# Sums over the keys in the first attention layer: one fp32 product per half against two fp32r passes taken one step later

## The chip, the cores and the metric

The kernel runs on one core of one Trainium2 chip. The metric is the device time of one execution in microseconds (us). A core has a matrix engine (TensorE, PE in the profile, its weight loads PEld), a vector engine (DVE), a scalar engine (ACT), GpSimd (POOL) and a queue that issues DMA (SP). Each runs its own list of instructions in order, and they meet at semaphores only.

## The reference, cut to what matters

Two layers, each a cross attention and a feed-forward part. The change lies in the first layer's cross attention, 16 batches, 56 queries, 16 heads (8 key heads), 1500 keys:

```
q = (layernorm(x) @ Wq); k = ctx @ Wk; v = ctx @ Wv           # heads of 128
scores = einsum('bhtd,bhsd->bhts', q, k) / sqrt(128)
attn = softmax(scores, axis=-1)                                # over the 1500 keys
x = x + einsum('bhts,bhsd->bhtd', attn, v) @ Wo
```

Everything is float32. The denominator of the softmax is the sum over the 1500 keys of exp(score - maximum).

## The kernel before

The layer's work on one batch is cut into 12 steps, one for each tile of 125 keys (t = 0 to 11). The 16 heads times 56 queries are 896 columns, handled in two halves of 448. The key and value projections are folded into the queries and the output weights, so that scores are products with the 128-wide context itself.

In step t of batch b, TensorE does, in this order: the scores of the next tile t+1, half 0 (four fp32r passes of 448 columns: L792 to L795, the last of them adds minus the row's maximum); some "side jobs"; the scores of tile t+1, half 1; more side jobs; the product of the probabilities of tile t with the context, half 0 (L804, one fp32 matmul that the profile shows as two records); side jobs; the same for half 1; the rest of the side jobs. The lists `STEPS` say which side jobs stand in a step. A job M (L826, one 448-column pass) makes scores of batch b+1 for the running maximum on DVE. The jobs N and A (L842 and L843, two 512-column passes) make norms that the second layer needs: DVE multiplies their result (L738); for N, POOL adds halves (L650) and DVE reduces (L747); for A, ACT adds up with four pairs of instructions (L552). Steps 0 and 1 have the jobs "MNMAMNMA", step 2 "NMAMNMA".

ACT, in its own list, does in step t first the exponentials of tile t+1 (`exp`, L570, one for each half, from PSUM to the buffer `probs`), then other work, and last the step's two `add_up`. POOL adds the probabilities of all tiles into `acc` (L641 for tiles 0 and 1, then L644).

When a batch is done, `acc` holds for each of 125 partitions the sums over its keys. `sums` (TensorE, L812) adds over the partitions with a matrix of ones, one fp32 matmul for each half. In the program half 0 of batch b-1 stands in step 0 of batch b behind the scores of half 1, and half 1 at the head of step 1. `sums_out` (ACT, L583) copies each half to `den`, the first in step 0 behind `exp`, the second behind the first `add_up` of step 0. Then DVE inverts in steps 3 to 10 and POOL multiplies.

Scores and sums share three PSUM banks, in the cyclic order of the list `ORDER` ("S" t half are scores, "D" sums, "-" is an empty turn):

```
ORDER = [("S", 0, 0), ("S", 0, 1), ("S", 1, 0), ("S", 1, 1), ("D", 0, 0), ("D", 0, 1), ("-", 0, 0)]
ORDER += [("S", t, half) for t in range(2, NT) for half in range(2)]
```

Entry i takes bank i mod 3. `wait_bank` makes TensorE wait until what stands three entries earlier has been read: by `exp` (semaphore `probs`) for scores, by `sums_out` (semaphore `den_out`) for sums.

In what follows S(t,h) are the scores of tile t, half h; D0 and D1 are the two sums; A2 and A3 are the two jobs A of step 1; N1 is the second job N of step 0.

Of the kernel before, what the change touches and what calls it, by code (L numbers as in the profile page):

```python
# [87 lines left out]

ORDER = [("S", 0, 0), ("S", 0, 1), ("S", 1, 0), ("S", 1, 1), ("D", 0, 0), ("D", 0, 1), ("-", 0, 0)]
ORDER += [("S", t, half) for t in range(2, NT) for half in range(2)]  # L90
assert len(ORDER) % 3 == 0

# [64 lines left out]
def before_attention(nc, m, a, tag, sem):  # L157

    s = semaphores(sem, tag, LN_SEMAPHORES + ["ld_x", "ld_mask", "ld_const", "ld_ident", "ld_w0", "ld_w0_rest", "ld_wq0", "ld_wq1", "ld_wq2", "ld_wq3", "ld_w1", "ld_land", "ld_nat", "const", "ready",
                 "on_act", "on_dve", "f_hi", "g_hi", "x_hi", "mcount", "ctx_hi", "q_hi", "ctx_lo", "kept",  # L160
                 "side_pe", "side_dve"])
    with ExitStack() as ctx:
# [87 lines left out]
        @block.gpsimd  # L250
        def _(pool):
            for i in range(NLOW):
                pool.wait_ge(s.ctx_hi, 1)
                cols = slice(S // NLOW * i, S // NLOW * (i + 1))
                pool.tensor_tensor(m.clo0[:, cols], m.land[:, cols], m.chi0[:, cols].bitcast(F32), ALU.subtract).then_inc(s.ctx_lo, 1)
            pool.wait_ge(s.q_hi, 1)
            pool.tensor_tensor(m.qlo0[:, :], q_first, m.qhi0[:, :].bitcast(F32), ALU.subtract).then_inc(s.kept, 1)
            pool.wait_ge(s.q_hi, 2)
            for part in range(NXQ):
                tiles = slice(NT // NXQ * part, NT // NXQ * (part + 1))  # L260
                to, x = m.xq0[:, tiles, :].bitcast(F32), nat[:, tiles, :]
                pool.tensor_tensor(to, x, to, ALU.subtract).then_inc(s.ctx_lo, 1)
                pool.wait_ge(s.ctx_lo, NLOW + 2 * part + 1)
                pool.tensor_tensor(to, to, x, ALU.add).then_inc(s.ctx_lo, 1)

        @block.vector
        def _(dve):
# [40 lines left out]
            def make_shift():  # L308

                dve.wait_ge(s.side_dve, len(PRE_SIDE))  # L310
                dve.wait_ge(s.ld_ident, 16)
                dve.tensor_tensor(m.shift0[:, :].rearrange("p (j c) -> p j c", c=TT),
                                  m.negmax[:, :].unsqueeze(2).to_broadcast([TT, QBLK, TT]),
                                  m.ident[0:TT, 0:TT].unsqueeze(1).to_broadcast([TT, QBLK, TT]),
                                  ALU.mult).then_inc(s.kept, 1)

# [124 lines left out]
def first_attention(nc, m, a, tag, sem):  # L441

    s = semaphores(sem, tag, [
        "ld_land", "ld_nat0", "ld_nat1", "ctx_hi", "ctx_lo", "q_hi", "q_lo", "nat_hi", "xq", "shift",
        "scores", "probs", "pv", "acc", "den", "den_out", "inv", "o_raw", "o_done",
        "ld_wv", "ld_wo", "side_pe", "side_dve", "side_act", "half_sum", "sum_dve", "sum_act", "rk_pre"])
    NP = 3
    with ExitStack() as ctx:
# [11 lines left out]
        top, negmax = m.top, m.negmax  # L460
        shift = [m.shift0, sb("shift1", [TT, QW], F32R)]
        prod = [sb(f"prod{i}", [KT, 4, C], F32) for i in range(NPROD)]
# [59 lines left out]
        def _(act):  # L522
# [50 lines left out]
            def values_out(b):  # L573
# [15 lines left out]
            for b in range(B):  # L589
                for t in range(NT):  # L590
                    for tile in tile_ahead(1, b, t):
                        exp(*tile)
                    if t == 0 and b > 0:
                        sums_out(b - 1, 0)
                        norms_out(b - 1)
                    if t == 2 and b + 1 < B:
                        nat_high(b + 1)
                    if t == NT - 1:
                        if b + 2 < B:
                            query_high(b + 2)  # L600
                            context_high(b + 2, 0)
                    for n in STEP_JOBS[b, t]:
                        if JOBS[n].kind == "A":
                            add_up(n)
                        if n == first_of(b, "A") and b > 0:
                            sums_out(b - 1, 1)
                        if JOBS[n].kind == "V":
                            i = JOBS[n].i
                            act.wait_ge(s.side_pe, n + 1)
                            act.activation(m.vo[:, 2 * i:2 * i + 2, :], side[n % 3][:, :], ACT.Copy).then_inc(s.side_act, 1)  # L610
                values_out(b)
                if b + 2 < B:
                    context_high(b + 2, 1)
# [7 lines left out]
        def _(pool):  # L621
# [46 lines left out]
            def make_shift(b):  # L668

                pool.wait_ge(s.side_dve, number(job_at("T", b, 1), "MTNA"))  # L670
                need(pool, s.scores, 2 * NT * (b - 1))
                pool.tensor_tensor(shift[b % 2][:, :].rearrange("p (j c) -> p j c", c=TT),
                                   negmax[:, :].unsqueeze(2).to_broadcast([TT, QBLK, TT]),
                                   m.ident[0:TT, 0:TT].unsqueeze(1).to_broadcast([TT, QBLK, TT]),
                                   ALU.mult).then_inc(s.shift, 1)

            for b in range(B):
                for t in range(NT):
# [103 lines left out]
        def _(pe):  # L782
            def scores_half(b, t, half):
# [10 lines left out]
                pe.matmul(out, chi[b % 2][:, keys], qhi[b % 2][:, cols], start=False, stop=False)  # L794
                pe.matmul(out, m.ones_r[:, :], shift[b % 2][:, cols], start=False, stop=True).then_inc(s.scores, 1)  # L795

# [51 lines left out]
            for b in range(B):  # L848
                for t in range(NT):
# [29 lines left out]
def second_attention(nc, m, a, tag, sem):  # L879

    s = semaphores(sem, tag, [
        "ld_land", "ld_nat0", "ld_nat1", "ctx_hi", "ctx_lo", "q_hi", "q_lo", "scores", "scaled", "probs", "pv", "pv_first", "acc",
        "acc_hi", "acc_lo", "den", "inv", "o_raw", "o_done", "fold_pe", "fold_act", "fold_dve", "y_pe", "y_act"])
    LAG, NP = 2, 3
    with ExitStack() as ctx:
# [43 lines left out]
        def _(act):  # L929
# [60 lines left out]
            for i in range(KC):  # L990
                act.wait_ge(s.y_pe, i + 1)
                act.activation(land[:, HALF * i:HALF * i + HALF], slots[:, 0, i, 0:HALF], ACT.Copy).then_inc(s.y_act, 1)

# [944 lines left out]
def build(nc, a, out):  # L1938
    with ExitStack() as ctx:
# [89 lines left out]
```

## Time and profile before

| | |
|---|---|
| median of 3 runs | 2083.45 us (2082.59 to 2083.99) |
| the profiled execution | 2081.46 us, span in the trace 2079.7 us |
| first attention layer in the trace | about 71 to 1155 us, batches of about 67.6 us |
| PE busy | 2051.3 us, 99% of the span |
| DVE, ACT, POOL busy | 1576.0 us (76%), 1208.0 us (58%), 1451.0 us (70%) |

A row of the timeline gives start and duration of an instruction in us, its engine, its line, what it writes and reads, its shape; in brackets the time that the engine sat idle before it and who ended that. Matmuls are pipelined: in a dense stream the durations overlap, and the cost of one is the distance from one end to the next.

### The profile page before, as it was taken

What the parts mean: (1) busy time and instruction counts of PE and PEld (TensorE: products, weight loads), DVE (VectorE), ACT (ScalarE), POOL (GpSimd) and SP (SyncE); (2) the same over time, 40 slices, a digit from 0 to 9 for tenths busy, and PEclk for the clock granted to TensorE, in tenths of its full rate; (3) what the DMA queues carried; (4) which work ended last, traced back from release to release, by engine and by line L of the source; (5) the groups of instructions that cost most, each with busy time, mean ns of one, the idle gap of its engine ahead of it and who ended that gap; (6) DMA issues with size and microseconds to landing.
All of it is one profiled execution on the core that took longest, in us unless ns stands there. A gap on an engine that the chain in (4) does not pass through costs nothing. (4 is left out here: it accounts for less than half of the span.)

```text
span 2079.7 us, 28199 instructions
## 1 busy us (share of the span) xinstructions
PE 2051.3 (99%) x8482; PEld 1520.4 (73%) x8482; DVE 1576.0 (76%) x2489; ACT 1208.0 (58%) x4201; POOL 1451.0 (70%) x1092
## 2 busy tenths in 40 slices
PE   8999999999999999999999989999999999999999
PEld 7777777777777777777777577666666666665998
DVE  4789988898889888898886677476766676752576
ACT  4676777767776777677767347544444444432433
POOL 1688888888888888888886254678787877851221
PEclk9999999999999999999999999999999999999999
DMA  4000000000000000000010410121211111001110
GB/s 138 30 16 17 30 30 16 30 16 31 30 16 16 31 31 16 17 30 30 16 43 9 137 58 1 45 60 31 59 33 57 41 49 48 28 0 54 46 51 22
DMA packets 15289, 75.68 MB, mean 36 GB/s; under 512 B 1762, under 2 KB 2258, under 8 KB 14130
## 3 DMA queue, kind: packets, MB, share of 16 engines
q1 hardware_dynamic: 15138, 73.89, 10.9%
q8 instruction: 68, 1.11, 0.2%
q14 instruction: 83, 0.68, 0.1%
HBM read 72.97 MB, written 0.92 MB: 36 GB/s over the span
## 5 line engine op out<-in xcount | busy, mean ns | idle before, releaser
L552 ACT ACTIVATE l_prod_act<-l_prod_act 125x128 f32<-125x128 f32 x1536 | 456.3, 298 | 298.6 <-DVE l_prod_act L738 293.5
L650 POOL TENSOR_TENSOR l_prod<-l_prod 125x256 f32<-125x256 f32 x384 | 280.3, 739 | 163.9 <-DVE l_prod L738 162.7
L1009 POOL TENSOR_TENSOR l_acc<-l_acc,l_probs 125x896 f32<-125x896 f32 x160 | 346.6, 2167 | 67.9 <-ACT l_probs L946 49.5
L946 ACT ACTIVATE l_probs<-l_scaled 125x896 f32<-125x896 f32 x192 | 182.8, 952 | 302.7 <-DVE l_scaled L1031 160.6
L1031 DVE TENSOR_TENSOR l_scaled<-l_slots,rk 125x896 f32<-125x896 f32 x192 | 206.9, 1084 | 180.9 <-PE l_slots L1107 180.7
L644 POOL TENSOR_TENSOR l_acc<-l_acc,l_probs 125x896 f32<-125x896 f32 x160 | 339.8, 2124 | 0.0
L552 ACT ACTIVATION_READ_ACCUMULATOR l_prod_act<-l_prod_act 125x1 f32 x1536 | 287.6, 187 | 0.0
L714 DVE SCALAR_TENSOR_TENSOR top<-l_side,mask_bias,top 125x448 f32<-125x448 f32 x330 | 217.4, 659 | 25.7 <-PE l_side L826 17.9
L570 ACT ACTIVATE l_probs<-l_slots,mask_bias 125x448 f32<-125x448 f32 x384 | 219.5, 617 | 1.2
L1105 PE MATMUL l_slots<-l_qhi,l_clo 128*125 128x448 f32 x384 | 203.0, 529 | 0.4
L842 PE MATMUL l_side<-norm_lo,l_chi 128*125 128x512 f32 x384 | 185.1, 482 | 0.1
L842 PE MATMUL l_side<-norm_lo,chi 128*125 128x512 f32 x384 | 180.9, 471 | 0.0
L804 PE MATMUL l_psO<-l_probs,spare 125*128 125x448 f32 x384 | 176.0, 539 | 0.0
L804 PE MATMUL l_psO<-l_probs,l_nat 125*128 125x448 f32 x384 | 176.0, 539 | 0.0
L738 DVE TENSOR_TENSOR l_prod<-l_side,xq 125x512 f32<-125x512 f32 x192 | 131.9, 687 | 50.7 <-PE l_side L843 49.0
L738 DVE TENSOR_TENSOR l_prod<-l_side,spare 125x512 f32<-125x512 f32 x192 | 131.8, 687 | 39.8 <-PE l_side L843 37.2
L1123 PE MATMUL l_psO<-l_probs,nat 125*128 125x448 f32 x384 | 160.5, 539 | 0.6 <-ACT qs L958 0.3
L1123 PE MATMUL l_psO<-l_probs,l_nat 125*128 125x448 f32 x384 | 160.3, 540 | 0.4
L747 DVE TENSOR_REDUCE l_msq<-l_prod 125x4 f32<-125x256 f32 x384 | 154.2, 408 | 0.0
L843 PE MATMUL l_side<-norm_hi,chi 128*125 128x512 f32 x384 | 151.4, 394 | 0.0
L843 PE MATMUL l_side<-norm_hi,l_chi 128*125 128x512 f32 x384 | 151.4, 394 | 0.0
L1106 PE MATMUL l_slots<-l_qlo,l_chi 128*125 128x448 f32 x384 | 140.6, 366 | 0.0
(277 smaller groups left out, 4952.3 us busy)
## 6 DMA issues: line engine op xcount, KB each, us to landing
land<-in_ctxT SPq DMA_DIRECT2D x32, 750.0 KB, 4.2
l_nat<-in_ctxN SPq DMA_DIRECT2D x16, 750.0 KB
post_we<-in_experts SPq DMA_DIRECT2D x20, 384.0 KB, 3.0
spare<-in_ctxN SPq DMA_DIRECT2D x8, 750.0 KB
nat<-in_ctxN SPq DMA_DIRECT2D x8, 750.0 KB
spare<-in_wo SPq DMA_DIRECT2D x2, 2048.0 KB, 7.4
spare<-in_wqT SPq DMA_DIRECT2D x4, 512.0 KB, 7.5
mid_fac<-in_factors SPq DMA_DIRECT2D x1, 2048.0 KB, 7.9
```

The lines of the kernel that those rows point to most:

```text
L552: last = act.activation(whole, whole, ACT.Copy, accum_out=msq[:, t, 4 * g + c:4 * g + c + 1])
L570: act.activation(P[t % NP][:, HALF * i:HALF * i + HALF], bank_of("S", t, i)[0:KT, 0:HALF], ACT.Exp, bias=m.mask_bias[:, b, t:t + 1]).then_ ...
L644: pool.tensor_tensor(acc[:, :], acc[:, :], P[t % NP][:, :], ALU.add).then_inc(s.acc, 1)
L650: pool.tensor_tensor(buf[:, :, 0:C // 2], buf[:, :, 0:C // 2], buf[:, :, C // 2:C], ALU.add).then_inc(s.half_sum, 1)
L714: dve.scalar_tensor_tensor(top[:, cols], bank, bias, top[:, cols], ALU.add, ALU.max).then_inc(s.side_dve, 1)
L738: dve.tensor_tensor(to[:, :, :], bank, xt.unsqueeze(1).to_broadcast([KT, 4, C]), ALU.mult).then_inc(s.side_dve, 1)
L804: last = pe.matmul(psO[:, half, 0:HALF], nat[b % 2][:, t, :], P[t % NP][:, cols], start=t == 0, stop=t == NT - 1)
L842: pe.matmul(bank[0:KT, :], chi[b % 2][:, keys], m.norm_lo[:, cols], start=True, stop=False)
L843: last = pe.matmul(bank[0:KT, :], chi[b % 2][:, keys], m.norm_hi[:, cols], start=False, stop=True)
L1009: pool.tensor_tensor(acc[:, :], acc[:, :], P[t % NP][:, :], ALU.add).then_inc(s.acc, 1)
L1031: dve.tensor_tensor(scaled[t % 2][:, :].rearrange("p (a h q) -> p a h q", a=2, q=QS), src, rk.to_broadcast([KT, 2, H // 2, QS]), ALU.mult) ...
L1123: last = pe.matmul(psO[:, half, 0:HALF], nat[par][:, t, :], P[t % NP][:, cols], start=t == 0, stop=t == NT - 1)
```

## The change

The sums of all batches but the last are made in another way. ACT copies `acc` rounded to fp32r (`sum_high`, L583 of the changed kernel) into `qlo` of the batch that is over, in step 0 behind `exp`. POOL subtracts the rounded part from `acc` into that batch's `shift` buffer (`sum_low`), at the end of its step 0. TensorE then multiplies ones with both parts, two fp32r passes for each half in place of one fp32 matmul. D0 moves from step 0 to step 1 (behind S(2,1)), D1 from the head of step 1 to the head of step 2. `sums_out` of half 0 stands in ACT's step 1 behind `exp`, that of half 1 at the head of ACT's step 2, ahead of `exp`. In `ORDER` the sums come after S(2,1). The matrix `ones_r` and the `shift` buffers grow to fit, two waits keep the buffers safe, and semaphores that nobody waited for are gone.

```diff
-ORDER = [("S", 0, 0), ("S", 0, 1), ("S", 1, 0), ("S", 1, 1), ("D", 0, 0), ("D", 0, 1), ("-", 0, 0)]
-ORDER += [("S", t, half) for t in range(2, NT) for half in range(2)]
+ORDER = [("S", t, half) for t in range(3) for half in range(2)] + [("D", 0, 0), ("D", 0, 1), ("-", 0, 0)]
+ORDER += [("S", t, half) for t in range(3, NT) for half in range(2)]
...
+            def sum_high(b):
+
+                act.wait_ge(s.acc, (NT - 1) * (b + 1))
+                act.wait_ge(s.scores, 2 * NT * (b + 1))
+                act.activation(qlo[b % 2][0:KT, :], acc[:, :], ACT.Copy).then_inc(s.sum_hi, 1)
+
...
+                    if t == 2 and b > 0:
+                        sums_out(b - 1, 1)
                     for tile in tile_ahead(1, b, t):
                         exp(*tile)
                     if t == 0 and b > 0:
+                        sum_high(b - 1)
+                        norms_out(b - 1)
+                    if t == 1 and b > 0:
                         sums_out(b - 1, 0)
-                        norms_out(b - 1)
...
-                        if n == first_of(b, "A") and b > 0:
-                            sums_out(b - 1, 1)
...
-                    need(pool, s.den, 2 * b)
+                    need(pool, s.sum_lo, b)
...
+            def sum_low(b):
+
+                pool.wait_ge(s.sum_hi, b + 1)
+                pool.tensor_tensor(shift[b % 2][:, :], acc[:, :], qlo[b % 2][0:KT, :].bitcast(F32), ALU.subtract).then_inc(s.sum_lo, 1)
...
+                    if t == 0 and b > 0:
+                        sum_low(b - 1)
...
-                pe.wait_ge(s.acc, (NT - 1) * (b + 1))
+                cols, out = slice(HALF * half, HALF * half + HALF), bank_of("D", 0, half)[:, 0:HALF]
                 wait_bank(pe, b + 1, "D", 0, half)
-                pe.matmul(bank_of("D", 0, half)[:, 0:HALF], m.ones[0:KT, :], acc[:, HALF * half:HALF * half + HALF],
-                          start=True, stop=True).then_inc(s.den, 1)
+                if b == B - 1:
+                    pe.wait_ge(s.acc, (NT - 1) * B)
+                    pe.matmul(out, m.ones[0:KT, :], acc[:, cols], start=True, stop=True).then_inc(s.den, 1)
+                    return
+                pe.wait_ge(s.sum_lo, b + 1)
+                pe.matmul(out, m.ones_r[0:KT, :], shift[b % 2][:, cols], start=True, stop=False)
+                pe.matmul(out, m.ones_r[0:KT, :], qlo[b % 2][0:KT, cols], start=False, stop=True).then_inc(s.den, 1)
...
-                    if t == 1 and b > 0:
+                    if t == 2 and b > 0:
                         sums(b - 1, 1)
                     for half in range(2):
                         for tile in tile_ahead(1, b, t):
                             scores_half(*tile, half)
-                        if half == 1 and t == 0 and b > 0:
+                        if half == 1 and t == 1 and b > 0:
                             sums(b - 1, 0)
```

The order of ACT's instructions around steps 0 to 2 of a batch, before: `exp` of tile 1 (L570), the two copies of sums (L583), the norms (L559), `add_up` (L552, x4 is one job A), `exp` of tile 2, two `add_up`, `exp` of tile 3.

```order
L570 ACTIVATE l_probs<-l_slots,mask_bias 125x448 x2
L583 ACTIVATE l_den<-l_slots 128x448
L559 ACTIVATE rk<-l_msq 125x192
L552 ACTIVATE l_prod_act,l_msq<-l_prod_act 125x128 x4
L583 ACTIVATE l_den<-l_slots 128x448
L552 ACTIVATE l_prod_act,l_msq<-l_prod_act 125x128 x4
L570 ACTIVATE l_probs<-l_slots,mask_bias 125x448 x2
L552 ACTIVATE l_prod_act,l_msq<-l_prod_act 125x128 x8
L570 ACTIVATE l_probs<-l_slots,mask_bias 125x448 x2
```

And in the changed kernel, where the copy of a sum is L589:

```order
L570 ACTIVATE l_probs<-l_slots,mask_bias 125x448 x2
L583 ACTIVATE l_qlo<-l_acc 125x896
L559 ACTIVATE rk<-l_msq 125x192
L552 ACTIVATE l_prod_act,l_msq<-l_prod_act 125x128 x8
L570 ACTIVATE l_probs<-l_slots,mask_bias 125x448 x2
L589 ACTIVATE l_den<-l_slots 128x448
L552 ACTIVATE l_prod_act,l_msq<-l_prod_act 125x128 x8
L589 ACTIVATE l_den<-l_slots 128x448
L570 ACTIVATE l_probs<-l_slots,mask_bias 125x448 x2
```

The second copy of a sum stood in step 0 between its two `add_up`; it now stands behind both `add_up` of step 1.

TensorE's instructions at the head of step 2 in the changed kernel, from the last side job of step 1 (with the semaphores waited for): D1 in two passes, S(3,0), one job N, S(3,1).

```order
L863 MATMUL l_side<-norm_lo,chi 125x512 [waits l0_side_dve]
L864 MATMUL l_side<-norm_hi,chi 125x512
L833 MATMUL l_slots<-l_shift,ones_r 128x448 [waits l0_sum_lo,l0_probs]
L834 MATMUL l_slots<-l_qlo,ones_r 128x448
L808 MATMUL l_slots<-qhi,clo 125x448 [waits l0_den_out]
L809 MATMUL l_slots<-qlo,chi 125x448
L810 MATMUL l_slots<-qhi,chi 125x448
L811 MATMUL l_slots<-shift,ones_r 125x448
L863 MATMUL l_side<-norm_lo,chi 125x512 [waits l0_side_dve]
L864 MATMUL l_side<-norm_hi,chi 125x512
L808 MATMUL l_slots<-qhi,clo 125x448 [waits l0_den_out]
```

The same place before, with other line numbers for the same work:

```order
L842 MATMUL l_side<-norm_lo,chi 125x512 [waits l0_side_dve]
L843 MATMUL l_side<-norm_hi,chi 125x512
L792 MATMUL l_slots<-qhi,clo 125x448 [waits l0_probs]
L793 MATMUL l_slots<-qlo,chi 125x448
L794 MATMUL l_slots<-qhi,chi 125x448
L795 MATMUL l_slots<-shift,ones_r 125x448
L842 MATMUL l_side<-norm_lo,chi 125x512 [waits l0_side_dve]
L843 MATMUL l_side<-norm_hi,chi 125x512
L792 MATMUL l_slots<-qhi,clo 125x448 [waits l0_probs]
```

S(3,0) and S(3,1) waited for exponentials and now wait for the copies of D0 and D1 (`den_out`).

## Rows read from the trace of the kernel before

**Rows 1.** The page: engines over the whole span, and the granted clock in 40 slices.

```profile
PE 2051.3 (99%) x8482; PEld 1520.4 (73%) x8482; DVE 1576.0 (76%) x2489; ACT 1208.0 (58%) x4201; POOL 1451.0 (70%) x1092
...
PEclk9999999999999999999999999999999999999999
```

**Rows 2.** Windows over batches 7 and 8: stretch, length, then busy time of each engine.

```profile
544.35:611.90 67.55, 67.55 (x277) 50.76 (x276) 59.95 (x107) 48.80 (x226) 57.56 (x52) 1.00 0.07 24
611.90:679.59 67.69, 67.69 (x278) 50.83 (x276) 59.95 (x107) 48.82 (x226) 57.59 (x52) 1.00 0.07 24
```

**Rows 3.** Timeline of PE, batch 7, from S(1,1) in step 0 to step 2.

```profile
546.46 0.37 PE L795 MATMUL l_slots<-l_shift,ones_r 112*125 112x448 f32 x1
546.67 0.92 PE L812 MATMUL l_slots<-l_acc,ones 125*128 125x448 f32 x2
547.08 0.71 PE L826 MATMUL l_side<-qhi,chi 128*125 128x448 f32 x1
...
553.79 0.36 PE L795 MATMUL l_slots<-l_shift,ones_r 112*125 112x448 f32 x1
...
557.26 0.40 PE L843 MATMUL l_side<-norm_hi,l_chi 128*125 128x512 f32 x1
...
558.57 0.40 PE L843 MATMUL l_side<-norm_hi,l_chi 128*125 128x512 f32 x1
```

**Rows 4.** Timeline of PE in the second layer: sums in two fp32r passes.

```profile
1865.24 0.37 PE L1138 MATMUL l_norm<-l_acc_lo,l_one 125*128 125x448 f32 x1
1865.44 0.36 PE L1139 MATMUL l_norm<-l_acc_hi,l_one 125*128 125x448 f32 x1
```

**Rows 5.** Timeline of DVE, step 0 of batch 7, and its product for A3.

```profile
546.80 0.68 DVE L738 TENSOR_TENSOR l_prod<-l_side,xq 125x512 f32<-125x512 f32 x1
...
549.26 0.68 DVE L714 SCALAR_TENSOR_TENSOR top<-l_side,mask_bias,top 125x448 f32<-125x448 f32 x1
549.86 0.68 DVE L738 TENSOR_TENSOR l_prod<-l_side,xq 125x512 f32<-125x512 f32 x1
...
557.93 0.68 DVE L738 TENSOR_TENSOR l_prod_act<-l_side,xq 125x512 f32<-125x512 f32 x1
```

**Rows 6.** Timeline of POOL, batch 7: the half sum of N1, the first addition.

```profile
550.62 0.73 POOL L650 TENSOR_TENSOR l_prod<-l_prod 125x256 f32<-125x256 f32 x1 [2.32 <-DVE l_prod L738]
552.00 2.13 POOL L641 TENSOR_TENSOR l_acc<-l_probs 125x896 f32<-125x896 f32 x1 [0.65 <-PE l_slots L812]
```

**Rows 7.** Timeline of ACT, batch 7: copies of the sums, A3's add_up, exp of tile 3.

```profile
549.49 0.54 ACT L583 ACTIVATE l_den<-l_slots 128x448 f32<-128x448 f32 x1
549.91 0.37 ACT L559 ACTIVATE rk<-l_msq 125x192 f32<-125x192 f32 x1
...
551.89 0.54 ACT L583 ACTIVATE l_den<-l_slots 128x448 f32<-128x448 f32 x1 [0.24 <-PE l_slots L812]
...
558.64 0.31 ACT L552 ACTIVATE l_prod_act<-l_prod_act 125x128 f32<-125x128 f32 x1 [1.65 <-DVE l_prod_act L738]
...
559.84 0.61 ACT L570 ACTIVATE l_probs<-l_slots,mask_bias 125x448 f32<-125x448 f32 x1
```

**Rows 8.** Groups by form: a 896-column copy on ACT, subtraction on POOL (mean ns).

```profile
L526 ACT ACTIVATE qhi<-qs 128x896 fp32r<-128x896 f32 x7 | 6.6, 942 | 0.0
...
L633 POOL TENSOR_TENSOR qlo<-qs,qhi 128x896 fp32r<-128x896 f32 x7 | 14.8, 2114 | 0.0
```

**Rows 9.** Timeline at two places where PE waited: for ACT's L610, for ACT's exp.

```profile
1150.18 0.57 ACT L610 ACTIVATE spare<-l_side 128x512 f32<-128x512 f32 x1
...
1150.81 0.18 PEld L842 LDWEIGHTS l_side<-norm_lo,l_chi 128*125 128x125 f32 x1 [0.82 <-ACT spare L610]
1150.81 0.49 PE L842 MATMUL l_side<-norm_lo,l_chi 128*125 128x512 f32 x1
...
74.12 0.47 PE L792 MATMUL l_slots<-qhi,clo 128*125 128x448 f32 x1
```

**Rows 10.** Timeline of PE between the layers: its longest idle time there.

```profile
1208.76 0.96 PE L1532 MATMUL mid_bk<-ident,mid_xn 112*128 112x112 f32 x8 [1.66 <-DVE mid_xn L1240]
```

More of the change, by code:

```diff
@@ L159, in before_attention @@
     s = semaphores(sem, tag, LN_SEMAPHORES + ["ld_x", "ld_mask", "ld_const", "ld_ident", "ld_w0", "ld_w0_rest", "ld_wq0", "ld_wq1", "ld_wq2", "ld_wq3", "ld_w1", "ld_land", "ld_nat", "const", "ready",
-                 "on_act", "on_dve", "f_hi", "g_hi", "x_hi", "mcount", "ctx_hi", "q_hi", "ctx_lo", "kept",
+                 "on_act", "on_dve", "f_hi", "g_hi", "x_hi", "mcount", "ctx_hi", "q_hi", "ctx_lo",
                  "side_pe", "side_dve"])
@@ L256, in _ @@
             pool.wait_ge(s.q_hi, 1)
-            pool.tensor_tensor(m.qlo0[:, :], q_first, m.qhi0[:, :].bitcast(F32), ALU.subtract).then_inc(s.kept, 1)
+            pool.tensor_tensor(m.qlo0[:, :], q_first, m.qhi0[:, :].bitcast(F32), ALU.subtract)
             pool.wait_ge(s.q_hi, 2)
@@ L311, in make_shift @@
                 dve.wait_ge(s.ld_ident, 16)
-                dve.tensor_tensor(m.shift0[:, :].rearrange("p (j c) -> p j c", c=TT),
+                dve.tensor_tensor(m.shift0[0:TT, :].rearrange("p (j c) -> p j c", c=TT),
                                   m.negmax[:, :].unsqueeze(2).to_broadcast([TT, QBLK, TT]),
                                   m.ident[0:TT, 0:TT].unsqueeze(1).to_broadcast([TT, QBLK, TT]),
-                                  ALU.mult).then_inc(s.kept, 1)
+                                  ALU.mult)
             dve.memset(m.ones[:, :], 1.0).then_inc(s.const, 1)
@@ L444, in first_attention @@
         "ld_land", "ld_nat0", "ld_nat1", "ctx_hi", "ctx_lo", "q_hi", "q_lo", "nat_hi", "xq", "shift",
-        "scores", "probs", "pv", "acc", "den", "den_out", "inv", "o_raw", "o_done",
+        "scores", "probs", "pv", "acc", "sum_hi", "sum_lo", "den", "den_out", "inv", "o_raw", "o_done",
         "ld_wv", "ld_wo", "side_pe", "side_dve", "side_act", "half_sum", "sum_dve", "sum_act", "rk_pre"])
@@ L460, in first_attention @@
         top, negmax = m.top, m.negmax
-        shift = [m.shift0, sb("shift1", [TT, QW], F32R)]
+        shift = [m.shift0, sb("shift1", [KT, QW], F32R)]
         prod = [sb(f"prod{i}", [KT, 4, C], F32) for i in range(NPROD)]
@@ L632, in query_low @@
                     pool.wait_ge(s.scores, 2 * NT * (b - 1))
+                    pool.wait_ge(s.den, 2 * (b - 1))
                 pool.tensor_tensor(qlo[b % 2][:, :], m.qs[:, b, :, :].rearrange("p h q -> p (h q)"),
@@ L671, in make_shift @@
                 need(pool, s.scores, 2 * NT * (b - 1))
-                pool.tensor_tensor(shift[b % 2][:, :].rearrange("p (j c) -> p j c", c=TT),
+                need(pool, s.den, 2 * (b - 1))
+                pool.tensor_tensor(shift[b % 2][0:TT, :].rearrange("p (j c) -> p j c", c=TT),
                                    negmax[:, :].unsqueeze(2).to_broadcast([TT, QBLK, TT]),
@@ L794, in scores_half @@
                 pe.matmul(out, chi[b % 2][:, keys], qhi[b % 2][:, cols], start=False, stop=False)
-                pe.matmul(out, m.ones_r[:, :], shift[b % 2][:, cols], start=False, stop=True).then_inc(s.scores, 1)
+                pe.matmul(out, m.ones_r[0:TT, 0:KT], shift[b % 2][0:TT, cols], start=False, stop=True).then_inc(s.scores, 1)
             def values_half(b, t, half):
@@ L882, in second_attention @@
         "ld_land", "ld_nat0", "ld_nat1", "ctx_hi", "ctx_lo", "q_hi", "q_lo", "scores", "scaled", "probs", "pv", "pv_first", "acc",
-        "acc_hi", "acc_lo", "den", "inv", "o_raw", "o_done", "fold_pe", "fold_act", "fold_dve", "y_pe", "y_act"])
+        "acc_hi", "acc_lo", "den", "inv", "o_raw", "o_done", "fold_pe", "fold_act", "fold_dve", "y_pe"])
     LAG, NP = 2, 3
@@ L991, in _ @@
                 act.wait_ge(s.y_pe, i + 1)
-                act.activation(land[:, HALF * i:HALF * i + HALF], slots[:, 0, i, 0:HALF], ACT.Copy).then_inc(s.y_act, 1)
+                act.activation(land[:, HALF * i:HALF * i + HALF], slots[:, 0, i, 0:HALF], ACT.Copy)
         @block.gpsimd
@@ L1966, in build @@
             for_first = lambda n, sh, dt: only.enter_context(nc.sbuf_tensor(n, sh, dt))
-            m.ones_r = for_first("ones_r", [TT, KT], F32R)
+            m.ones_r = for_first("ones_r", [C, C], F32R)
             m.mask_bias = for_first("mask_bias", [KT, B, NT], F32)
@@ L1974, in build @@
             m.top, m.negmax = for_first("top", [KT, QW], F32), for_first("negmax", [TT, QBLK], F32)
-            m.shift0 = for_first("shift0", [TT, QW], F32R)
+            m.shift0 = for_first("shift0", [KT, QW], F32R)
             m.xq = for_first("xq", [KT, NT, C], F32)
```

## The prediction, made before the changed kernel ran

> **What bounds the kernel now.** I read the page first. TensorE is busy for 99% of the span and the granted clock stands in its top tenth throughout, which is the 2.4 GHz level [rows 1]. The windows over two batches of the first layer show the same closer: 67.55 us of PE in 67.55 us, 67.69 in 67.69, against at most 59.95 on DVE, 57.6 on POOL and 48.8 on ACT [rows 2]. So in this stage a microsecond of TensorE's own work that goes is a microsecond gained, but a microsecond in which TensorE waits is also lost, since it has no other slack to take it from. The timelines of one batch (batch 7; the two windows show how alike batches are) then say who would be late where.
>
> I count TensorE by ends. S(1,1) ends at 546.46 + 0.37 = 546.83. The side job behind the sum ends at 547.08 + 0.71 = 547.79 and is itself one pass [rows 3]. A pass of 448 columns in a stream costs 0.20 [rows 4]. That leaves 547.79 - 0.20 - 546.83 = 0.76 for the fp32 sum; I use 0.75.
>
> **What the change takes away.** Two passes of 0.20 and 0.21 come in place of 0.75: a sum of this very shape, 125x448 with ones, stands in the second layer at that spacing [rows 4]. I take 0.41 for both, so 0.34 is saved on each half. There are 15 batches with two halves: 30 x 0.34 = **10.2 us less**. With the ends read 0.04 otherwise it is 9 to 11.4.
>
> What this price would be by a rule: the Trainium skill ("FP8 and Floating Point Precision", TensorE Precision Notes) says a true fp32 product takes four passes through the array. Four passes at this trace's 0.204 would be 0.82, the saving 0.41 a half and 12.3 us in all. The row gives 0.76, so the rule counts a little too much here, and the sum goes by the row.
>
> POOL's first addition waited for the old sum, 0.65 us [rows 6]; POOL was idle there and this frees nothing on TensorE.
>
> **What it adds on ACT and POOL.** The copy of `acc` on ACT has the size of one at 0.94 us, POOL's subtraction the size of one at 2.11 [rows 8]. Neither engine is the bound: POOL goes from 57.6 to 59.7 in a batch of 67.6. What matters is when they end. If no one waited, they would cost nothing. ACT trades a copy of 0.54 for 0.94 in step 0.
>
> **First new wait: D0 for the low part.** TensorE wants D0 right behind S(2,1). Before, S(2,1) ended at 553.79 + 0.36 = 554.15 [rows 3]; with the two fp32 sums ahead of it gone, 554.15 - 1.50 = 552.65. The low part needs two things. First, the high part: ACT begins it at 549.49, where the copy of D0 stood [rows 7], and ends it 0.94 later, 550.43. Second, POOL must be through with the half sum of N1, which stands ahead in its list. Before, DVE's product for N1 began at 549.86 and ended at 550.54, and POOL began at 550.62 [rows 5, 6]. Now TensorE brings N1 0.75 earlier, but DVE has a chain of its own: the product at 546.80 and then M1, A0, M2, N1, back to back at 0.60 each (549.26 to 549.86) [rows 5]. So N1's product begins at 546.80 + 4 x 0.60 = 549.20, ends at 549.88; POOL's half sum runs from 549.96 to 550.69, and the subtraction to 550.69 + 2.11 = 552.80. That is later than the 552.65 at which TensorE comes.
>
> What a wait costs beyond its length shows where TensorE waited before. ACT's L610 ended at 1150.75, the weight load and the matmul began at 1150.81; behind exp a 448-column pass took 0.47 from there [rows 9]. So the first pass ends 0.06 + 0.47 = 0.53 behind the end of its producer, against 0.20 in a stream. D0's first pass: 552.80 + 0.53 = 553.33 in place of 552.85, **0.48 lost** per batch. Bounds: if DVE has no backlog, the low part is 0.2 earlier, and 0.3 is lost; if POOL is 0.2 later, 0.7. If the copy alone decided, 550.43 + 2.11 + 0.53 = 553.07, still 0.22 lost; nothing is lost only if the end of the low part comes 0.5 earlier than I reckon.
>
> **Second new wait: S(3,1) for the copy of D1.** This is the large one. In `ORDER` S(3,0) now comes three entries behind D0 and S(3,1) three behind D1, so both wait for `den_out`. S(3,0) is safe: D0 ends near 553.5; ACT copies it when it has done, from 550.43 on, the norms (0.37), two `add_up` (1.20 each, 558.64 to 559.84) and two halves of exp (0.61 each) [rows 7], so by 555.0 with the copy itself, while TensorE wants the bank after 557. For S(3,1), ACT must have copied D1 out, and in ACT's list that copy stands behind both `add_up` of step 1. The second of these belongs to A3, the last side job of step 1. All the work from A3 on is therefore in series. Before, A3 ended on TensorE at 557.26 + 0.40 = 557.66; DVE multiplied from 557.93; ACT's `add_up` began at 558.64 and the next instruction of ACT, exp, at 559.84 [rows 3, 5, 7]. That is 2.18 behind the end of A3. The copy takes this place and lasts 0.54 [rows 7], S(3,1)'s first pass ends 0.53 behind it: 2.18 + 0.54 + 0.53 = 3.25 behind A3. D1 itself is long done, 0.41 behind A3, so it is only the copy's place in ACT's list that matters.
>
> TensorE would need much less: from A3's end to the end of the job N behind S(3,0) it took 558.57 + 0.40 - 557.66 = 1.31 [rows 3]. With D1 (0.41) ahead and the first pass of S(3,1) (0.20), 1.92. **Lost: 3.25 - 1.92 = 1.33** per batch. The wait is tied to the same batch's A3 and not to how early TensorE is, so the 0.7 gained before does not cover it. Bounds: the chain behind A3 depends on DVE's backlog; with the product begun at once, 0.05 behind A3 rather than 0.27, the loss is 1.1; with 0.2 more on ACT it is 1.5.
>
> While it waits, TensorE's own later work is queued behind: a job M and A, the values of tile 2, and so all of step 2. exp of tile 3 comes behind the copy and is 0.54 late against A3, but its first consumer is in step 3. Nothing of this gives time back, because TensorE stays dense after it.
>
> A rule that speaks for less: the Trainium skill ("TensorE: Matmul & The Clock Gate", Step-by-step) says TensorE pulls weight loads ahead of matmuls in flight. If it did so ahead of a wait, the load would be over and a pass would end in about 0.37 in place of 0.47, 30 x 0.10 = 3 us less lost in all. At the wait in rows 9 the weight load itself begins only when ACT has ended, so the trace does not bear that out for a load whose matmul waits, and I keep 0.47.
>
> **The sum.** Per batch -0.68 + 0.48 + 1.33 = +1.13; 15 of them are +17.0. The last of these has no M jobs and is a little different (its step 1 is shorter, so D0 comes sooner against the low part); I add 0.3 for it: **+17.3 us**. Against the profiled execution, 2081.46 + 17.3 = 2098.8. The median of the runs lies 2.0 above that execution, 2083.45, so I say 2100.7 for the runs. The wider `ones_r` fill, the dropped semaphores and the bounds of the other instructions lie in the preamble and beside other work, or are no work: nothing.
>
> **The rivals.**
>
> Only the saving counts (ends on the other side). One mechanism: the copy of D1 gets ahead of TensorE. It does if ACT reaches it by 1.92 - 0.53 - 0.54 = 0.85 behind A3, where the rows say 2.18; and the low part is in time. Time: 2083.45 - 10.2 = 2073.2. For it speaks that the list entry "-" and the steps leave the banks much room elsewhere; against it, ACT's list in the order shown, in which both `add_up` stand ahead. I give it 0.07.
>
> Only S(3,1) waits; the low part is in time because DVE's or POOL's chain in step 0 is half a microsecond shorter than reckoned. -10.2 + 15 x 1.33 = +9.8: 2093.2. For it: the margin is 0.15 of bare time plus the restart. Against: even ACT's copy alone would leave 0.22. Chance 0.13, the near half of it inside my range.
>
> The second wait is about half of what I reckon (ACT's `add_up` for A3 overlaps more), 0.65 a batch: the sum is then -10.2 + 15 x (0.3 + 0.65) = +4, within reach of no change if the first is nothing. Chance 0.06.
>
> More is late: POOL's 2.11 us pushes its additions and half sums, DVE waits for half sums, TensorE for DVE, another 0.5 a batch: +24.8, 2108. POOL had 0.65 and 2.32 idle in step 0 and 1 [rows 6], which takes the 2.11 up; or the clock falls after waits of over 1 us. Against the clock: TensorE sat 1.66 idle between the layers and the granted clock stayed up [rows 1, 10]. Chance 0.08.
>
> Both waits as reckoned: 0.66.
>
> **How the numbers follow.** The likeliest gives 2100.7; with its bounds (losses 1.1 and 0.3 to 1.5 and 0.7, saving 9 to 11.4) it runs from 2083.45 + 21.3 - 11.4 = 2093.4 to 2083.45 + 33.3 - 9 = 2107.8. The range 2093 to 2106 takes these ends almost whole and half of the case with one wait; outside are the other side, the halved wait and the worse case, some 0.2. A change within 0.2%, 4.2 us, is about what a measurement of this kernel can't tell from none. Slower by more: 0.66 + 0.13 + 0.08 and part of the halved case, 0.89; same 0.04; faster 0.07.
>
> **What would show it.** Right: PE's passes of the sums 0.20 apart, twice 30 of them; in each batch a PE idle time ahead of the first pass of S(3,1) (L808) with ACT's copy L589 as its end, about 1.3 us of lost end-to-end time, 15 times, and a short one ahead of D0 (L833) that POOL's subtraction ends; batches of some 68.7 us. Wrong: no wait at L808 and batches of 66.9 would mean that the copy of D1 is earlier than ACT's list lets me think. No wait at L833 alone would mean that DVE's chain in step 0 is shorter. If the time went up by over 25, a wait elsewhere, on DVE's side banks or on POOL, would have to show.

## The result

The change makes the kernel slower: 2106.5 us median (2102.8 to 2107.0, 4 runs) against 2083.0 us (2081.4 to 2084.0, 4 runs), ratio 1.0107 with a 95% interval of 1.0095 to 1.012. The medians are 23.5 us apart, 20 to 25 us by the interval, where I had said 17.3. The 2106.5 stands at the very top of my range of 2093 to 2106: half a microsecond above it as a time, and just inside it by the ratio (1.0107, where 2106 over the 2083.45 that I reckoned from is 1.0108). The profiled execution took 2106.46 us, with a span of 2104.6 us.

The profile's page for the changed kernel says little: TensorE is busy for 6 us more, 98% of the span in place of 99%.

```profile
PE 2057.4 (98%) x8482; PEld 1519.0 (72%) x8482; DVE 1576.2 (75%) x2489; ACT 1219.0 (58%) x4216; POOL 1481.4 (70%) x1107
```

Windows cut at the ends of the values' products show where the time went. Columns: stretch, length, busy time (and number of instructions) of PE, PEld, DVE, ACT, POOL, granted clock, DMA share, GB/s. First the kernel before, steps 0, 1, 2 and 3 to 11 of batch 7:

```profile
544.05:550.43 6.38, 6.38 (x27) 4.67 (x26) 5.69 (x12) 6.03 (x23) 4.08 (x5) 1.00 0.26 99
550.43:556.99 6.56, 6.56 (x28) 4.85 (x27) 5.13 (x9) 5.37 (x27) 4.51 (x4) 1.00 0.05 21
556.99:562.61 5.62, 5.62 (x25) 4.30 (x24) 5.02 (x10) 3.97 (x15) 4.48 (x4) 1.00 0.01 3
562.61:611.60 48.99, 48.99 (x204) 36.94 (x203) 44.11 (x80) 33.44 (x165) 44.50 (x39) 1.00 0.05 17
```

Then the changed kernel, the same four stretches of batch 7, and the whole of batches 7 and 8, which answer to [rows 2]:

```profile
554.55:560.57 6.02, 6.02 (x24) 4.13 (x24) 5.60 (x12) 5.76 (x21) 4.07 (x5) 1.00 0.26 94
560.57:567.21 6.64, 6.45 (x27) 4.76 (x27) 5.12 (x9) 5.81 (x29) 6.32 (x5) 1.00 0.07 31
567.21:574.56 7.35, 6.31 (x27) 4.59 (x26) 5.09 (x10) 5.04 (x20) 4.67 (x5) 1.00 0.01 2
574.56:623.57 49.01, 49.01 (x203) 36.94 (x203) 44.15 (x80) 32.89 (x161) 44.51 (x39) 1.00 0.05 17
554.55:623.57 69.02, 67.78 (x277) 50.43 (x277) 59.97 (x108) 49.50 (x227) 59.56 (x53) 1.00 0.07 23
623.57:692.62 69.05, 67.85 (x278) 50.49 (x277) 59.95 (x108) 49.53 (x227) 59.61 (x53) 1.00 0.07 23
```

Steps 3 to 11 have not changed by more than 0.02 us. The batch is 69.03 us on the mean of the two in place of 67.62: +1.41 us, 15 times, is 21.2. (The sums are remade 15 times, once for each batch that has a predecessor.) Step by step: step 0 lost an fp32 product of 0.75 and is only 0.36 shorter; step 1 had 0.75 taken away and 0.41 put in, and is 0.08 longer; step 2 had 0.41 put in and is 1.73 longer. So TensorE lost 0.39 + 0.42 + 1.32 us in three places, of which I had named two.

The timeline of PE in the changed kernel, batch 7, shows the places (L847 is a side job M, L863 and L864 are a side job's passes, L820 the values, L811 the end of scores, L833 and L834 a sum, L808 the start of scores):

```profile
557.16 0.37 PE L847 MATMUL l_side<-qhi,chi 128*125 128x448 f32 x1
557.43 0.49 PE L863 MATMUL l_side<-norm_lo,l_chi 128*125 128x512 f32 x1
557.77 0.40 PE L864 MATMUL l_side<-norm_hi,l_chi 128*125 128x512 f32 x1
558.16 0.99 PE L820 MATMUL l_psO<-l_probs,l_nat 125*128 125x448 f32 x2
...
563.17 0.36 PE L811 MATMUL l_slots<-l_shift,ones_r 112*125 112x448 f32 x1
563.73 0.45 PE L833 MATMUL l_slots<-shift,ones_r 125*128 125x448 f32 x1 [0.19 <-POOL shift L657]
564.01 0.36 PE L834 MATMUL l_slots<-qlo,ones_r 125*128 125x448 f32 x1
...
567.71 0.37 PE L833 MATMUL l_slots<-shift,ones_r 125*128 125x448 f32 x1
567.92 0.37 PE L834 MATMUL l_slots<-qlo,ones_r 125*128 125x448 f32 x1
...
569.18 0.40 PE L864 MATMUL l_side<-norm_hi,l_chi 128*125 128x512 f32 x1
570.62 0.47 PE L808 MATMUL l_slots<-l_qhi,l_clo 128*125 128x448 f32 x1 [1.04 <-ACT l_den L589]
```

ACT and POOL in the same stretch: the copy of the values, the rounded copy of `acc`, A3's `add_up`, the copy of D1; N1's half sum and the subtraction.

```profile
557.03 0.98 ACT L577 ACTIVATE qs<-l_psO,valid 128x896 f32<-128x896 f32 x1
...
559.98 0.94 ACT L583 ACTIVATE qlo<-l_acc 125x896 fp32r<-125x896 f32 x1
...
568.86 0.31 ACT L552 ACTIVATE l_prod_act<-l_prod_act 125x128 f32<-125x128 f32 x1 [1.65 <-DVE l_prod_act L754]
...
570.05 0.52 ACT L589 ACTIVATE l_den<-l_slots 128x448 f32<-128x448 f32 x1
```

```profile
560.75 0.74 POOL L663 TENSOR_TENSOR l_prod<-l_prod 125x256 f32<-125x256 f32 x1 [1.96 <-DVE l_prod L754]
561.44 2.14 POOL L657 TENSOR_TENSOR shift<-l_acc,qlo 125x896 fp32r<-125x896 f32 x1
```

Read from the end of one matmul to the end of the next. **S(3,1):** the copy of D1 ends at 570.57, L808 starts at 570.62 and ends at 571.09; in a stream it would have ended at 569.58 + 0.20, so 1.31 is lost. **D0:** the subtraction ends at 563.58, L833 starts at 563.73 and ends at 564.18 in place of 563.53 + 0.20: 0.45. **Step 0, values of tile 0:** ACT's copy of the last batch's values out of the same PSUM ends at 558.01; the product ends at 559.15, and not at 558.17 + 0.75 = 558.92: 0.23. Just before, the side job's first pass ends at 557.92 and not at 557.53 + 0.23 = 557.76: 0.16. The weight loads name what ended two of these waits, DVE's first M (L727) at 557.43 and ACT's copy of D1 (L589) at 570.62. At 558.13 the view names only the issue, so that the copy of the values ended that wait is read from the times alone; e2 tests it:

```profile
557.43 0.18 PEld L863 LDWEIGHTS l_side<-norm_lo,l_chi 128*125 128x125 f32 x1 [0.29 <-DVE top L727]
558.13 0.30 PEld L820 LDWEIGHTS l_psO<-l_probs,l_nat 125*128 125x128 f32 x2 [0.41 <-issue]
...
570.62 0.18 PEld L808 LDWEIGHTS l_slots<-l_qhi,l_clo 128*125 128x125 f32 x1 [1.49 <-ACT l_den L589]
```

And the view of waits over the first layer says that it is every batch that has a predecessor (in total, times, longest):

```profile
PEld l_slots L808 <- ACT l_den L589: 21.9, 15, 1.5
PEld l_slots L833 <- issue: 8.3, 15, 0.9
PEld l_psO L820 <- issue: 6.7, 15, 1.0
```

Read in the same way in all 15 batches, D0 loses 0.42 to 0.45 us and S(3,1) 1.28 to 1.32 in the first 14. In the last one, which has no M jobs, they lose 0.76 and 1.17.

The two profiled executions are 24.9 us apart (spans of 2104.6 and 2079.7). Most of the 3.7 us beyond 21.2 does not lie in the changed steps. The last section has it.

### The profile page after: what moved, and what is told of

It is laid out like the page before. It is cut to its first block and busy times, and to the rows that moved or that the text cites. A ratio compares the mean times of both kernels' runs of the same rounds, so it can differ in the third digit from the quotient of the medians.

```text
span 2104.6 us, 28244 instructions
## 1 busy us (share of the span) xinstructions
PE 2057.4 (98%) x8482; PEld 1519.0 (72%) x8482; DVE 1576.2 (75%) x2489; ACT 1219.0 (58%) x4216; POOL 1481.4 (70%) x1107
## 5 line engine op out<-in xcount | busy, mean ns | idle before, releaser
L552 ACT ACTIVATE l_prod_act<-l_prod_act 125x128 f32<-125x128 f32 x1536 | 456.1, 298 | 304.5 <-DVE l_prod_act L754 299.3
L552 ACT ACTIVATION_READ_ACCUMULATOR l_prod_act<-l_prod_act 125x1 f32 x1536 | 287.5, 187 | 0.0
L570 ACT ACTIVATE l_probs<-l_slots,mask_bias 125x448 f32<-125x448 f32 x384 | 219.6, 617 | 9.8 <-PE l_slots L811 9.7
L863 PE MATMUL l_side<-norm_lo,l_chi 128*125 128x512 f32 x384 | 185.7, 484 | 0.1
L863 PE MATMUL l_side<-norm_lo,chi 128*125 128x512 f32 x384 | 181.4, 472 | 0.0
L820 PE MATMUL l_psO<-l_probs,l_nat 125*128 125x448 f32 x384 | 176.5, 540 | 0.6 <-ACT qs L577 0.6
L820 PE MATMUL l_psO<-l_probs,spare 125*128 125x448 f32 x384 | 176.5, 541 | 0.0
L763 DVE TENSOR_REDUCE l_msq<-l_prod 125x4 f32<-125x256 f32 x384 | 154.5, 409 | 0.0
L864 PE MATMUL l_side<-norm_hi,chi 128*125 128x512 f32 x384 | 151.5, 394 | 0.0
L864 PE MATMUL l_side<-norm_hi,l_chi 128*125 128x512 f32 x384 | 151.3, 394 | 0.0
```

Of the source, the lines that this page charges most:

```text
L552: last = act.activation(whole, whole, ACT.Copy, accum_out=msq[:, t, 4 * g + c:4 * g + c + 1])
L570: act.activation(P[t % NP][:, HALF * i:HALF * i + HALF], bank_of("S", t, i)[0:KT, 0:HALF], ACT.Exp, bias=m.mask_bias[:, b, t:t + 1]).then_ ...
L820: last = pe.matmul(psO[:, half, 0:HALF], nat[b % 2][:, t, :], P[t % NP][:, cols], start=t == 0, stop=t == NT - 1)
L863: pe.matmul(bank[0:KT, :], chi[b % 2][:, keys], m.norm_lo[:, cols], start=True, stop=False)
L864: last = pe.matmul(bank[0:KT, :], chi[b % 2][:, keys], m.norm_hi[:, cols], start=False, stop=True)
```

## The experiments

Eight kernels, each timed in five rounds beside the kernel before (2082.6 us median in the first four, 2083.4 with the last four).

**e1, the copy of D1.** D1 is made in step 1, ahead of the second half of the values, and copied out between the two `add_up` of step 1.

```diff
-                    if t == 2 and b > 0:
-                        sums_out(b - 1, 1)
...
                             add_up(n)
+                            if t == 1 and b > 0 and JOBS[n].i == 2:
+                                sums_out(b - 1, 1)
...
-                    if t == 2 and b > 0:
-                        sums(b - 1, 1)
...
+                    if t == 1 and b > 0:
+                        sums(b - 1, 1)
                     values_half(b, t, 1)
```

> The changed kernel with one difference: D1 is made in step 1, ahead of the second half of the values of tile 1, and ACT copies it out between the two add_up of step 1; S(3,1) then finds its bank free. My theory (the place of D1's copy in ACT's list costs 1.31 us per batch, 15 times): 19.7 us less than the changed kernel, batches of 67.7 us in place of 69.03, about 2085 to 2087 us. Rival (the loss comes from the extra copy on ACT and the extra subtraction on POOL, wherever the sums stand): no difference, 2103 to 2107 us. No idle time of PE that ends by L589 should be left.

Measured: 2086.9 us (2084.5 to 2087.5), ratio 1.0017 (1.0008 to 1.0026). Steps 1 and 2 and the whole of batch 7:

```profile
551.27:558.31 7.04, 6.86 (x29) 5.15 (x29) 5.52 (x10) 6.21 (x30) 6.72 (x6) 1.00 0.06 27
558.31:563.93 5.62, 5.62 (x24) 4.30 (x24) 4.71 (x9) 4.09 (x15) 4.31 (x4) 1.00 0.01 3
...
545.24:612.92 67.68, 67.49 (x278) 50.51 (x277) 59.97 (x108) 49.41 (x227) 59.59 (x53) 1.00 0.07 24
```

Step 2 is back at 5.62, step 1 has taken over the 0.41 of the product. 1.34 us of batch 7 (1.27 of batch 8) and 19.6 us of the median went with the place of D1 and its copy; the product had to move with the copy, which reads it. ACT and POOL do the same work (49.41 and 59.59 us busy against 49.50 and 59.56). The rival, that the additional work costs in itself wherever the sums stand, is out.

**e2, the copy of the values.**

```diff
+                        if t == NT - 1 and JOBS[n].kind == "A" and JOBS[n].i == NBLK_A - 1:
+                            values_out(b)
                         if JOBS[n].kind == "A":
                             add_up(n)
...
-                values_out(b)
                 if b + 2 < B:
                     context_high(b + 2, 1)
```

> The changed kernel with one difference: ACT copies out the values of a batch ahead of the last add_up of step 11 and not behind it. Theory (with D0 gone from step 0, the first values product of step 0 waits for this copy, 0.23 us of 0.39 lost there, the other 0.16 a wait for DVE): step 0 is 0.2 to 0.4 us shorter, 3 to 6 us less than the changed kernel, about 2100 us. Rival (step 0 is longer than reckoned because the fp32 sum that was there cost only 0.35 us): no difference.

Measured: 2100.6 us (2099.2 to 2105.3), ratio 1.0092 (1.0076 to 1.0107). This interval overlaps with the changed kernel's (1.0095 to 1.012), and the medians are 5.9 us apart where the trace gives 3 (0.21 a batch, 15 times). So the time alone does not size this step; the trace does. Step 0 is 5.80 in place of 6.02 us:

```profile
551.44:557.24 5.80, 5.80 (x25) 4.22 (x24) 5.60 (x12) 5.80 (x21) 4.10 (x5) 1.00 0.26 94
```

These 0.22 us are the wait for the copy, read above as 0.23; the 0.16 for DVE stays.

**e3, the low part.** ACT rounds `acc` ahead of `exp`, and POOL subtracts ahead of its half sum for N1.

```diff
+                    if t == 0 and b > 0:
+                        sum_high(b - 1)
                     for tile in tile_ahead(1, b, t):
                         exp(*tile)
                     if t == 0 and b > 0:
-                        sum_high(b - 1)
                         norms_out(b - 1)
...
                             halve(n)
-                    if t == 0 and b > 0:
-                        sum_low(b - 1)
+                            if t == 0 and b > 0 and JOBS[n].i == 0:
+                                sum_low(b - 1)
```

> The changed kernel with two moves: ACT makes the rounded copy of acc ahead of exp of tile 1, and POOL subtracts ahead of its half sum for the second job N of step 0. Theory (D0 waits for the low part, 0.45 us lost per batch): step 1 is 0.45 us shorter, 6.7 us less than the changed kernel, about 2098 to 2100 us, and L833 has no idle time before it. Rival (the wait at D0 is paid back at S(3,1), whose wait ends by ACT's copy at a time that does not depend on D0): no difference. Theory says that wait hangs on A3, which moves with D0, so all of it is gained.

Measured: 2099.7 us (2097.9 to 2100.3), ratio 1.0081 (1.0067 to 1.0095). Step 1 and step 2:

```profile
557.53:563.74 6.21, 6.21 (x27) 4.85 (x27) 5.13 (x9) 5.81 (x29) 5.93 (x5) 1.00 0.07 31
563.74:571.06 7.32, 6.28 (x26) 4.58 (x26) 5.09 (x10) 5.03 (x19) 4.44 (x4) 1.00 0.01 2
```

Step 1 gains 0.43 and step 2 stays (7.32 against 7.35): the wait at S(3,1) hangs on A3 of the same batch and does not eat what is gained ahead of it.

**e4, all three.** The moves of e1, e2 and e3 together.

> All three moves of the runs before at once. Theory: the waits are gone and the saving of 0.68 us per batch is left, less at most 0.16 for the side bank that DVE holds in step 0: 7.8 to 10.2 us less than the kernel before, 2073 to 2076 us, batches of 66.95 to 67.1 us. Rival (ACT's and POOL's additional work costs in itself): 2083 or more.

Measured: 2074.5 us (2073.0 to 2075.3), ratio to the kernel before 0.9961 (0.9948 to 0.9973): 8 us faster than before, and the best kernel of this study.

```profile
541.00:546.79 5.79, 5.79 (x24) 4.21 (x24) 5.59 (x12) 5.79 (x21) 4.84 (x6) 1.00 0.27 96
546.79:553.40 6.61, 6.61 (x29) 5.22 (x29) 5.54 (x10) 6.08 (x30) 6.03 (x6) 1.00 0.08 33
553.40:559.02 5.62, 5.62 (x25) 4.30 (x24) 4.72 (x9) 4.08 (x15) 4.24 (x4) 1.00 0.01 3
...
541.00:608.03 67.03, 67.03 (x277) 50.66 (x277) 60.00 (x108) 49.30 (x227) 59.63 (x53) 1.00 0.07 24
608.03:675.10 67.07, 67.07 (x277) 50.72 (x277) 59.96 (x108) 49.35 (x227) 59.67 (x53) 1.00 0.07 24
```

A batch is 67.05 on the mean of the two, 0.57 below 67.62. The saving of 0.68 less the 0.16 of DVE's side bank, which no move touches, would be 0.52: they agree to 0.05.

**e5, a control: the kernel before with e2's move.**

> The kernel before with one difference: ACT copies the values of a batch out ahead of the last add_up of step 11. Theory (the fp32 sum D0 in step 0 hid the wait for this copy, so there was none): no difference, 2081 to 2084 us, step 0 stays 6.38 us. Rival (the copy cost TensorE time before too, and the gain of the same move in the changed kernel has nothing to do with D0): some 3 us less.

Measured: 2083.4 us (2081.6 to 2085.1), ratio 0.9998 (0.9989 to 1.0007), step 0 at 6.38. The copy of the values costs nothing as long as the fp32 product of D0 stands ahead of the values:

```profile
546.84:553.22 6.38, 6.38 (x26) 4.68 (x26) 5.69 (x12) 6.29 (x25) 4.07 (x5) 1.00 0.26 100
```

**e6 and e7, the price of the product with and without a wait behind it.** Both have one fp32 product of the rounded part for each pair of passes; e6 is otherwise the changed kernel, e7 is otherwise e4. They leave the low part out of the denominators, so they serve to price the product only.

```diff
-                pe.matmul(out, m.ones_r[0:KT, :], shift[b % 2][:, cols], start=True, stop=False)
-                pe.matmul(out, m.ones_r[0:KT, :], qlo[b % 2][0:KT, cols], start=False, stop=True).then_inc(s.den, 1)
+                pe.matmul(out, m.ones[0:KT, :], qlo[b % 2][0:KT, cols].bitcast(F32), start=True, stop=True).then_inc(s.den, 1)
```

> The changed kernel with each pair of passes of a sum replaced by one fp32 product of ones and the rounded part; the low part stays out of the denominators, its subtraction and the waits stay. Theory: D0 costs 0.34 us more per batch, D1 stands ahead of the wait for its own copy, which hangs on A3's add_up and not on D1, so D1's 0.34 is hidden: 5.1 us more than the changed kernel (batches of 69.37 us), 2108 to 2111 us. Rival (TensorE's own work counts everywhere): 10.2 us more, batches of 69.7, 2113 to 2116 us.

> The kernel with all three moves, again with one fp32 product of the rounded part for each pair of passes (the low part stays out of the denominators). Theory: there is no wait there that could hide it, so both halves count, 0.68 us per batch, 10.2 us more than with two passes: about 2084 to 2085 us, batches of 67.7 us. Rival (the two passes save less than 0.34 a half in place): less than that.

Measured: e6 2109.9 us (2109.3 to 2110.7), ratio 1.0125 (1.0112 to 1.0139), e7 2085.1 us (2083.3 to 2087.4), ratio 1.0007 (0.9998 to 1.0016). First e6, steps 1 and 2; then e7, step 1 and the whole batch:

```profile
561.70:568.68 6.98, 6.79 (x27) 4.78 (x27) 5.12 (x9) 5.91 (x29) 6.57 (x5) 1.00 0.05 22
568.68:576.03 7.35, 6.63 (x27) 4.61 (x26) 5.09 (x10) 5.04 (x19) 4.44 (x4) 1.00 0.01 2
```

```profile
551.94:559.26 7.32, 7.32 (x29) 5.24 (x29) 5.56 (x10) 6.21 (x30) 6.37 (x6) 1.00 0.06 27
...
546.15:613.85 67.70, 67.69 (x277) 50.74 (x277) 59.97 (x108) 49.41 (x227) 59.56 (x53) 1.00 0.07 24
```

In e6 step 1 is 0.34 longer, step 2 is 7.35 as in the changed kernel though its product is 0.34 longer: behind it TensorE waits anyway. e6's batches are 69.36 and 69.38 us, 0.34 longer. In e7 both products count: 7.32 against 6.61 in step 1, which holds both. So the saving that the change was to bring is real and of the size reckoned, and in the changed kernel the half that D1 saves was spent on a longer wait.

**e8, DVE's last reductions behind the first M of the next batch.** The edit is made on e4.

```diff
                         side_job(n)
+                        if at == 0 and t == 0 and b > 0:
+                            for i in range(NBLK - LAG_N, NBLK):
+                                add_up(b - 1, i)
...
-                    if t == NT - 1:
+                    if t == NT - 1 and b == B - 1:
```

> The kernel with all three moves, and DVE's last three reductions of a batch put behind the first M of the next one and not ahead of it. Theory (0.16 us of step 0 is TensorE waiting for the side bank that this M holds): step 0 is 5.63 in place of 5.79 us, 2.4 us less, 2071 to 2073 us. Rival (N1's product comes later by the reductions, or N0's bank is late in turn): no gain or a wait at a later side job of step 0.

Measured: 2076.5 us (2074.6 to 2078.5), ratio 0.9964 (0.9952 to 0.9977): not told apart from e4 by time. The 5.63 us expected for step 0 did not come: it is 5.93 in place of 5.79, and the batches are 67.16 and 67.20 in place of 67.03 and 67.07, so the trace says slightly worse. The rival was right: the reductions now stand ahead of N0's product on DVE, and TensorE waits for the side banks of N0 and M1 in turn.

```profile
546.24 0.18 PEld L852 LDWEIGHTS l_side<-qhi,chi 128*125 128x125 f32 x1 [0.37 <-DVE l_prod L756]
546.83 0.18 PEld L868 LDWEIGHTS l_side<-norm_lo,l_chi 128*125 128x125 f32 x1 [0.41 <-DVE top L729]
```

## Why the prediction was right, and what it missed

**What the change takes away** (0.34 a half, 10.2 us): 0.69 a batch by e7 against e4, (7.32 + 5.60) - (6.61 + 5.62) in steps 1 and 2, and 10.5 us between their medians (9.7 when each is taken against the kernel before timed beside it). The four passes that the Trainium skill ("FP8 and Floating Point Precision", TensorE Precision Notes) gives a true fp32 product would have made it 0.82; that counts too much here too.

**First new wait, D0 for the low part** (0.48): 0.45 in the trace, 0.43 by e3. The order of releases was as reckoned: POOL waited for DVE's product of N1 and not for ACT's copy. But that the size fits so well is partly luck. Counted from the end of S(1,1) (546.83 before, 557.33 now, 10.50 later), S(2,1) ended at 553.03 and the low part at 553.08, where I had 552.65 and 552.80: 0.38 and 0.28 too early. Both errors come in the main from one source, the step that failed (below). DVE ran out of work for 0.22 us ahead of M2, which TensorE brought late, and N1's product began 0.29 later than I reckoned. In the difference they nearly cancel:

```profile
559.39 0.68 DVE L730 SCALAR_TENSOR_TENSOR top<-l_side,mask_bias,top 125x448 f32<-125x448 f32 x1 [0.22 <-PE l_side L847]
559.99 0.68 DVE L754 TENSOR_TENSOR l_prod<-l_side,xq 125x512 f32<-125x512 f32 x1
```

**Second new wait, S(3,1) for the copy of D1** (1.33): 1.31 in the trace, 1.27 to 1.34 by e1. This is the step that decides the sign, and it could be read from ACT's list: a copy put at the head of a step stands behind the `add_up` of the step before, which wait for TensorE's last job there.

**The first pass behind a wait** (0.53 behind its producer's end): 571.09 - 570.57 = 0.52 behind ACT, 564.18 - 563.58 = 0.60 behind POOL, 0.08 later than behind ACT. In all 15 batches it is 0.52 or 0.53 behind ACT and 0.58 to 0.60 behind POOL. The weight load began only at the release: at S(3,1) load and matmul both begin at 570.62, and the load's idle time of 1.49 us is ended by ACT's L589. So the load was not pulled ahead of this wait either.

**What was missing.** The mechanism that I forecast was right, and the sum was short by one term that I had put at nothing. The step that failed is "with the two fp32 sums ahead of it gone, 554.15 - 1.50": it takes for granted that step 0 gets shorter by the whole 0.75. I priced what the change puts in new places and did not ask what the product had covered in its old one. It stood between S(1,1) and the first values product, and ACT's copy of the last batch's values ended just there. The kernel before, timeline of ACT in batch 7:

```profile
546.54 0.99 ACT L577 ACTIVATE qs<-l_psO,valid 128x896 f32<-128x896 f32 x1
```

It ends at 547.53; S(1,1), M and A without the sum end at 546.83 + 0.20 + 0.47 = 547.50, and in a stream the values follow at once. The cost is 0.39 a batch, 5.8 us: 0.23 of it the copy (e2, e5), 0.16 the side bank of M0, which DVE reaches only behind three reductions (L763, 1.06 us from 555.72). That 0.16 was not undone by an experiment: e8 moved the wait and did not remove it. So its cause is read from the trace (the load that L727 ends) and not shown by a run. With this term my sum is 17.3 + 5.8 = 23.1. That it falls within 0.4 of the 23.5 between the medians is again partly luck: the changed batches explain 21.2, and some 3 us of the profiled execution lie elsewhere, in two falls of the clock (last section), of which the prediction has nothing. The one run of the changed kernel at a mean clock of 1.000 took 2102.8 us, 19.8 above the median of the kernel before.

Of the rivals, "only the saving counts" came true in e4 alone, after three moves and with 0.57 in place of 0.68 us a batch.

## What to carry to other kernels

When the bounding engine has no slack, a matmul that is removed or moved was also time in which other engines finished something: look at what the next instruction behind it waits for, and when that ends today. Before a copy out of PSUM is put at the head of a step, ask what the instructions ahead of it in the copying engine's list wait for: e1 gained 19.6 us by putting D1's copy ahead of one `add_up`, with D1 itself moved up to be ready for it. When a wait is found, count from the instruction on which it hangs; gains ahead of that instruction are kept (e3), and work put between it and the wait is free as long as it is shorter than the wait (e6: 0.34 us).

## What the runs showed of the hardware

TensorE's clock fell to the lower of its two levels late in the changed kernel's profiled execution, in a stage that the change does not touch. The engine had been busy without a break since 1951.14; before that it had waited 1.20 us for DVE. Just ahead of the fall stood a row of 32 narrow matmuls from 1955.86 on (the view below was cut at 1957.5 and shows the last 17). Then eight passes of 448 columns end 0.37 apart in place of 0.20; with the part passes on either side, the ten from 1959.63 to 1962.90 lost 1.5 us. From 1963.21 on the passes are 0.20 apart again:

```profile
1957.26 1.82 PE L1954 MATMUL post_bk<-post_wr,post_xnT 128*112 128x16 f32 x17
...
1960.29 0.57 PE L1896 MATMUL post_bk<-post_xhi,post_whi 128*128 128x448 f32 x1
1960.66 0.57 PE L1894 MATMUL post_bk<-post_xhi,post_wlo 128*128 128x448 f32 x1
```

The profiled execution of the kernel before has a clock of 1.00 over that stage. So has e4, although TensorE waited the same 1.20 us for DVE in it (to 1918.92); in e8's the clock of the 10 us from 1925 is 0.83. There was a second fall early on: between 20 and 40 us the mean clock is 1.00 before and 0.91 in the changed kernel, where 24 small matmuls (L406, from 21.42) took 4.33 us against 2.95 before. TensorE had waited 1.60 and 0.95 us just ahead of them, and 1.28 and 0.94 before:

```profile
20.00:40.00 20.00, 19.05 (x106) 17.83 (x105) 10.56 (x22) 7.96 (x14) 3.85 (x4) 0.91 0.14 51
```

The first layer's scores begin at 72.8 us there and at 70.8 before. Of the changed kernel's four runs three have a mean clock of 0.998 and took 2106.5 to 2107.0 us; the one at 1.000 took 2102.8. The kernel before shows the same spread: of its 36 runs beside the experiments those at 1.000 took 2081.1 to 2083.2 us, those at 0.997 or 0.998 2085.4 to 2086.0. Why the clock falls in some executions and not in others stays open: nothing here was tried on it. Whether the change makes it likelier is open too. Of the ten profiled executions the late fall is in six, all with the new sums (the changed kernel, e1, e2, e6, e7, e8), and not in e3 and e4, which have them too; the early one is in the changed kernel, in e6 and in e5, which has the old sums. Runs of one kernel lie 1 to 6 us apart, so differences of a few microseconds in all were read from the batches of the trace rather than from the medians.
